# TensorE's loops written out as straight code in a decoder layer; the other engines keep theirs

## What is computed

```python
# self-attention, one head: the row sums of the causal exp(scores) go through a small network
q, k = rope(x @ Wq.T), rope(x @ Wk.T)                     # bfloat16
o = where(causal, exp(q @ k.T / 512 ** 0.5), 0).sum(-1)
a = relu(o[..., None] @ fc1_w.T + fc1_b) @ fc2_w.T + fc2_b
x = layernorm(x + a)
# cross-attention: 16 heads of 32, 154 keys, a bias for each head, query and key
w = softmax((split(x) @ split(ctx).T + bias) / 32 ** 0.5)
x = layernorm(x + merge(w @ split(ctx)) @ w_out)
# feed-forward 512 -> 2048 -> 512; weights quantised to 8 bits by row or column, x and hidden to 16
h = gelu(quant16(x) @ quant8(W_in) + b_in)
x = layernorm(x + quant16(h) @ quant8(W_out) + b_out)
```

## Time and profile before

| | us |
|---|---|
| median of 3 runs | 2375.98 |
| lowest, highest | 2374.82, 2393.3 |
| the profiled execution | 2373.34 |
| its span from the first to the last instruction | 2371.8 |
| TensorE busy with matmuls | 2138.6 (90%), 11904 instructions |
| VectorE busy | 1783.0 (75%) |
| ScalarE busy | 1083.4 (46%) |
| GpSimdE busy | 818.4 (35%) |
| mean granted share of TensorE's clock | 0.941 |

### The profile page before, as it was taken

How to read it: one execution, slowest core, us unless ns; L and a number is a source line. 1 busy time by engine, 2 the same in 40 slices (tenths; PEclk the granted TensorE clock), 3 DMA queues, 4 the chain that set the end, 5 groups by cost and what they waited for, 6 DMA issues and landing times. The chain is left out here.

```text
span 2371.8 us, 37044 instructions
## 1 busy us (share of the span) xinstructions
PE 2138.6 (90%) x11904; PEld 1168.3 (49%) x11904; DVE 1783.0 (75%) x3345; ACT 1083.4 (46%) x1522; POOL 818.4 (35%) x819
## 2 busy tenths in 40 slices
PE   7999999975999989999999728999998869999997
PEld 3444444431876667667677513444443334444443
DVE  6769586855777988888899644966665378888885
ACT  1444444443544545445455213344443365555551
POOL 2212222321244445445455621222222124334332
PEclk9999999996789999899899959999999989999999
DMA  6334343457899669759855248877789656666662
GB/s 224 121 118 136 118 135 103 120 133 187 204 170 227 184 153 218 211 161 176 246 158 134 81 152 284 242 254 261 253 268 251 242 177 231 230 222 232 224 233 80
DMA packets 386907, 447.83 MB, mean 189 GB/s; under 512 B 279462, under 2 KB 279750, under 8 KB 368352
## 3 DMA queue, kind: packets, MB, share of 16 engines
q1 hardware_dynamic: 322736, 286.14, 44.0%
q0 software_dynamic: 64048, 160.28, 21.4%
HBM read 259.00 MB, written 138.73 MB: 168 GB/s over the span
## 5 line engine op out<-in xcount | busy, mean ns | idle before, releaser
L1668 PE MATMUL ps_h<-xT,w 128*128 128x512 f16 x2048 | 455.9, 385 | 28.5 <-DMA xT<-x_lo 22.2
L1908 PE MATMUL ps<-w,g_hi 128*128 128x512 f16 x1024 | 389.1, 380 | 29.8 <-DVE g_lo L1846 29.8
L1908 PE MATMUL ps<-w,g_lo 128*128 128x512 f16 x1024 | 388.9, 380 | 0.0
L1668 PEld LDWEIGHTS ps_h<-xT,w 128*128 128x128 f16 x2048 | 202.1, 99 | 276.4 <-issue 27.8
L1499 ACT ACTIVATE h<-ps_h,b_in_sb,col_scale 128x512 f32<-128x512 f32 x256 | 197.7, 777 | 270.8 <-PE ps_h L1668 239.4
L1237 PEld LDWEIGHTS ps_o<-vm,pT 128*128 128x128 f32 x2048 | 303.4, 205 | 12.9
L1059 DVE TENSOR_REDUCE stack<-ps_m 128x2 f16<-128x308 f32 x512 | 242.7, 476 | 77.3 <-PE ps_m L1191 52.2
L1237 PE MATMUL ps_o<-vm,pT 128*128 128x33 f32 x2048 | 287.1, 266 | 0.0
L1017 ACT ACTIVATE pT<-logit 128x512 f32<-128x512 f32 x320 | 198.8, 624 | 171.6 <-DVE logit L1077 171.6
L1575 DVE TENSOR_REDUCE amax_t<-h 128x1 f32<-128x2048 f32 x64 | 146.1, 2283 | 134.7 <-ACT h L1499 133.8
L1189 PE MATMUL ps_m<-kb,q_heads 128*128 128x308 f16 x512 | 163.9, 320 | 46.3 <-DVE stack L1059 27.6
(11 more groups left out here) (176 smaller groups left out, 3918.4 us busy)
## 6 DMA issues: line engine op xcount, KB each, us to landing
hidden<-h POOLq DMA_DIRECT2D x64, 1024.0 KB, 7.2
hT<-hidden SPq DMA_DIRECT2D x64, 1024.0 KB, 6.6
xc<-x_cols SPq DMA_DIRECT2D x16, 1024.0 KB, 5.0
xr<-x_rows SPq DMA_DIRECT2D x16, 1024.0 KB, 5.5
x_rows<-x POOLq DMA_DIRECT2D x16, 1024.0 KB, 4.8
x1t<-x_rows SPq DMA_DIRECT2D x64, 256.0 KB, 3.4
bt_main<-bias_main SPq DMA_DIRECT2D x16, 1024.0 KB, 6.5
xres<-x_rows SPq DMA_DIRECT2D x64, 256.0 KB, 3.8
```

Of the source, the lines that this page charges most:

```text
L1668: mm = pe.matmul(ps_h[f % 4][:], w1[:, c, f * P:(f + 1) * P], xT[:, e, a, :, c, :], start=(a == 0 and c == 0), stop=(a == 1 and c == KC - 1))
L1908: mm = pe.matmul(ps[t][:], g[:, e, f, t * P:(t + 1) * P], w2[:, f, :], start=(f == 0 and a == 0), stop=(f == FC - 1 and a == 1))
```

## The change

TensorE's loops become Python loops, so that each iteration is written into the program as code of its own. That holds for all four of TensorE's: `over_steps` and `over_quarters` get a twin that takes no engine and is called by TensorE alone, and the two `Fori` of the feed-forward passes become `range`. The order of the matmuls, what they compute, which semaphores are waited for and at which values stay the same. The counter is a plain number now, so all of TensorE's thresholds are constants. No other engine's program changes.

```diff
+        def over_steps_unrolled(step):
+
+            step(-1, BLOCKS - 1)
+            for j in range(BLOCKS):
+                step(0, j)
+            for b in range(1, BATCH - 1):
+                for j in range(BLOCKS):
+                    step(b, j)
+            for j in range(BLOCKS):
+                step(BATCH - 1, j)
+            step(BATCH, 0)
...
-            over_steps(pe, step)
+            over_steps_unrolled(step)
...
+        def over_quarters_unrolled(quarter):
+
+
+            for q in range(-8, 16):
+                quarter(q // 4, q % 4, (q // 4) % 2)
+            for m in range(2, UNITS // 2 - 1):
+                for e in range(2):
+                    for i in range(4):
+                        quarter(2 * m + e, i, e)
+            for q in range(QUARTERS - 8, QUARTERS + 9):
+                quarter(q // 4, q % 4, (q // 4) % 2)
...
-            over_quarters(pe, quarter)
+            over_quarters_unrolled(quarter)
...
-                with pe.Fori(1, NBLK // 2 - 1) as m:
+                for m in range(1, NBLK // 2 - 1):
                     blk(2 * m, 0)
                     blk(2 * m + 1, 1)
...
-                with pe.Fori(1, NBLK // 2 - 1) as m:
+                for m in range(1, NBLK // 2 - 1):
                     blk(2 * m, 0)
                     blk(2 * m + 1, 1)
```

## The result

The time went up: 2433.06 us as the median of 4 runs (2414.34 to 2488.5) against 2384.01 for the kernel before on the same chip (4 runs, 2374.82 to 2393.3), a ratio of 1.0219 with a 95% interval of 1.0162 to 1.0276. A second set on another chip gave 1.0185 (1.0085 to 1.0284). The prediction, no change, was wrong. The profiled execution of after took 2414.34 us with a span of 2412.8, 41.0 more than before's.

A forecast was written before the change was run, and what follows sets the result against it. TensorE, busy 90%, was taken to bound the kernel, its back-edge stalls being VectorE's. Terms of 0 + 0 + 0 on the profiled 2373.3 us, set beside the runs' median of 2376.0, gave 2375 us, range 2358 to 2393.

The forecast's parts named there:

- What bounds the kernel, and whose stall it is: Whole kernel: TensorE bounds, busy 90%; time lost at back-edges, 42.4 us in all, is from VectorE crossing its own.
- five long steps: Behind back-edges: one self-attention step of 34.0 us against 26.4, four cross-attention quarters of 20.0 against 11.3; forecast to stay.
- Rival B: Attention stages: TensorE's own back-edges are what costs, so 42.4 us go, giving 2333 us; chance 5%.
- Part 1: All four TensorE loops: 15 taken branches go, hidden under matmuls already queued; worth 0 us, bound -42.4 us.
- part 2: TensorE's looped steps: waits against a computed count become waits against a constant; 0 us, bounds -4.8 and +4.8.
- Part 3: TensorE's code fetch: 96 packets instead of 49, 0.4 to 1.2 us each, in time; 0 us, upper bound 55 us.
- rival C: First feed-forward pass: added fetches make a transpose late, 4.6 us a block, 55 us, 2430; two or three blocks 2385; 7%.
- Part 4: Other engines' loops stay, and with them VectorE's back-edge losses of 7.6 + 4 x 8.7 us.
- rival D: Cross-attention: phase shift of VectorE against GpSimdE, 32 x 0.4 = 13 us less, 2362, or 3 us more; chance 8%.

The follow-up runs named there:

- early2: Transposes of x issued at block's start, xb loads moved to ScalarE except blocks 2 and 3; on the changed kernel 0.9992, on the kernel before 0.9975.
- pad256: Changed kernel with 256 already met waits more on TensorE at the start of the first feed-forward pass; 0.9983 to the kernel before.
- all_but_ff1: Kernel before with three of TensorE's loops written out, that of the first feed-forward pass kept a loop; 0.9995 to the kernel before.

## Why the prediction was wrong

- **What bounds the kernel, and whose stall it is**: right. TensorE's own back-edges cost nothing. The five long steps are all there without them: 20.7 us in the row above, 19.8, 22.6 and 19.8 for the other three quarters, 33.6 us for the step that took 34.0. Rival B is out.
- **Part 1 (branches), part 2 (constant waits)**: right, 0 us. Quarters of 11.3 and 11.0 and blocks of 27.60 are unchanged, and early2 looped and written out differ by under 2 us in the pass.
- **Part 3, the number of packets**: right, 95 against 96 foreseen, and 0.2 us of idle time of TensorE on issue in the whole run; every packet came in time for TensorE.
- **Part 3, their cost**: the step that failed. It took "0 us" because TensorE was not kept waiting by its code. The packets' effect on others was left to rival C, and there it was mis-sized. C said "the fetch adds 0.4 to 1.2 us to one DMA engine" and "where it bites TensorE stands 1.2 us". The packet does take about 1 us, but the pairs for blocks 5, 7, 9, 11 and 13 landed 4 to 21 us later than before's, in pair 9 with all sixteen steps of its semaphore. TensorE stood 6.6, 11.5, 1.2, 11.9, 9.2 and 17.7 us ahead of blocks 3, 5, 7, 9, 11 and 13, 58.1 together, where before had 5.7 there and 6.7 ahead of block 14. A disturbance was priced by the disturbing transfer's length, not by what the disturbed one did.
- **Rival C's place and condition**: right. It named the transposes of the first pass, waits for xT beyond five and a falling clock; 8 waits and 75 us at the lower clock within the pass (before 29) came. The 6.8 us that it took from the earlier trace rows as the price of one late transpose is the wait ahead of block 0, at the pass's start; the late ones in before cost 5.1 (block 3) and 6.7 (block 14). Its price for all twelve looped blocks, 55 us, lies near the 53 us of the pass only because too small a price was set against too many blocks; with "most of it 2385 to 2400" the text took two or three blocks.
- **The argument against C**: "blocks 1 to 3 and 14 to 15 ran with fetches". In before one pair met a packet in the harmful part of its life, that for block 3, 5.3 us behind its issue: it landed after 24 us and TensorE waited 5.1 us. The row was read as acquittal when it was a hint. The others of those blocks prove nothing: most packets fell elsewhere, and the pair for block 4 had one 6.8 us behind its issue but had all but landed by then (9.7 us). The pair for block 14 was late (27 us, 6.7 us of waiting) without any.
- **The chance**: C had 7%. A spare time of 0.4 to 2.9 us in blocks 6 to 13, and none in block 5, was to be had from the same trace, by setting the landing of each pair against the next block's start. The earlier trace rows gave only the median (12.0) and maximum (18.4) of a landing, which against 27.6 us looks roomy; they do not count the 7 us before the pair is issued nor the first transpose.
- **Part 4 and rival D**: VectorE's stalls stayed. Phase shifts within cross-attention exist, with the first pass starting anywhere from 1392 to 1422 us, but they follow neither kernel. D's own sum is too large: quarters of 11.3 and 11.0 us give 32 x 0.3 = 10 us, not 13.

The Trainium skill ("Runtime: NRT & Kernel Launch", section "Instruction fetch mechanics") describes code as coming in 16-KiB blocks over a DMA queue of the engine's own and calls the cost mostly hidden. The blocks are in the trace, 95 packets with 1.56 MB. Hidden holds for TensorE itself, which stood 0.2 us on issue, but not for the other transfers: 1.0219 and 1.0225 at one phase against 0.9983 at another.

## What to carry to other kernels

Before adding traffic of any kind, code included, find the transfer with the least room, measured from the moment it is needed backwards and block by block, and ask at what moment of its life the new packets fall; a median duration hides that. If a change of code size slows a stage whose instructions did not change, shift the code by some idle instructions: a loss that comes and goes with the shift is one of phase. What took the loss away here was an earlier issue of the transfer with the least room (7 us, by taking a wait out of its queue), not the choice of loop or straight code; how much of that is room and how much the packet's new moment is not shown.

## What the hardware showed that was not expected

- One 16-KB code packet of about 1 us, 4.8 to 6.4 us behind the issue of a pair of DMA transposes, went with a landing after 22 to 38 us (once 18) instead of 18 to 21; sixteen ordinary 16-KB packets at that moment, each 0.6 to 1.3 us, with 32 to 46 us; one ordinary packet with 18 to 23 us in nearly all blocks. Code packets 13 us or more behind the issue cost no time that the runs show, though single pairs were late there too (26.1 and 27.5 us in pad256).
- In a late pair the transposes' packets of some 250 B take 62 ns in the mean instead of 21, and the DMA queues move 151 GB/s where the same part of an undisturbed block moves 357, at shares of 1.22 and 1.12. Why transposes suffer so much more than the packet's own length stays open.
- Late pairs also come without any such packet: the pair for block 14 of before (27 us), and every second one in the profiled execution of all_but_ff1 (24 to 28 us).
- A loop body of 672 matmuls and as many weight loads, written out so that TensorE takes no branch, is worth nothing: 11.30 us a quarter either way.
- Met waits on one semaphore are put two to an instruction, so 512 of them, not 256, make up a 16-KB packet.
